# Routed experts computed in split bf16, with the weights split during the dense attention

## The reference, cut to what matters

```
x = x + dense cross attention(layernorm(x), context of 4 x 1601 rows; 16 query heads, 4 KV heads of 128)
x = x + (routed experts + shared expert)(layernorm(x))
x = x + window attention(layernorm(x))
x = x + fp8 feed forward(layernorm(x))
```

```
scores = sigmoid(x @ gate_w); the best 2 of 4 groups of experts, in these the best 6 of 32 experts for each token
xs = the 1024 * 6 rows of x, sorted by expert
g = ragged_dot(xs, w_gate); u = ragged_dot(xs, w_up)          # 256 x 176 for each expert
d = ragged_dot(silu(g) * u, w_down)                           # 176 x 256 for each expert
out = sum over the 6 experts of a token, weighted, + silu(x @ sw_gate) * (x @ sw_up) @ sw_down
```

## Time and profile before

| what | value |
|---|---|
| median of 3 executions | 1865.14 us (1864.81 to 1865.66) |
| the profiled execution | 1864.89 us, span 1862.8 us |
| PE busy, share of the span | 1710.4 us, 92% |
| DVE | 1405.2 us, 75% |
| ACT | 1103.7 us, 59% |
| POOL | 1100.0 us, 59% |

### The profile page before, as it was taken

How to read it: one execution, slowest core, us unless ns; L and a number is a source line. 1 busy time by engine, 2 the same in 40 slices (tenths; PEclk the granted TensorE clock), 3 DMA queues, 4 the chain that set the end, 5 groups by cost and what they waited for, 6 DMA issues and landing times. The chain is left out here.

```text
span 1862.8 us, 41598 instructions
## 1 busy us (share of the span) xinstructions
PE 1710.4 (92%) x14581; PEld 1314.5 (71%) x14727; DVE 1405.2 (75%) x3734; ACT 1103.7 (59%) x2798; POOL 1100.0 (59%) x1718
## 2 busy tenths in 40 slices
PE   4799999999999999999999999986999999589987
PEld 3578777788787787877787887765555555339974
DVE  7898886888877878888788788756656665575746
ACT  6576777676777667777676666652134333173534
POOL 5578695786866958868568577510266664181210
PEclk8899999999999999999999999996999999796998
DMA  3211111011010100110001000325389996500100
GB/s 126 75 52 30 61 39 50 19 36 47 18 39 19 37 20 18 59 32 19 19 19 36 24 1 24 122 92 220 101 253 269 275 267 188 189 15 24 43 9 26
DMA packets 69529, 140.24 MB, mean 75 GB/s; under 512 B 10921, under 2 KB 38674, under 8 KB 69074
## 3 DMA queue, kind: packets, MB, share of 16 engines
q1 hardware_dynamic: 58514, 105.37, 18.3%
q0 software_dynamic: 9984, 30.42, 4.8%
q10 hardware_dynamic: 832, 1.84, 0.3%
HBM read 111.73 MB, written 25.86 MB: 74 GB/s over the span
## 5 line engine op out<-in xcount | busy, mean ns | idle before, releaser
L920 DVE TENSOR_TENSOR att_pT<-att_pT 128x512 bf16<-128x512 f32 (+1 forms) x512 | 320.9, 650 | 166.2 <-ACT att_pT L729 163.1
L565 PE MATMUL att_out<-att_V,att_pT 128*128 128x128 bf16 x5760 | 386.8, 219 | 13.9 <-DVE att_pT L920 12.0
L565 PEld LDWEIGHTS att_out<-att_V,att_pT 128*128 128x128 bf16 x5760 | 349.0, 98 | 40.8 <-DVE att_pT L920 24.3
L729 ACT ACTIVATE att_pT<-att_pT 128x512 bf16<-128x512 f32 (+1 forms) x512 | 278.0, 572 | 128.8 <-PE att_pT L551 128.8
L735 ACT ACTIVATE att_prob<-att_scores,att_negmax 128x512 f32<-128x512 f32 (+1 forms) x512 | 330.3, 655 | 17.5 <-DVE att_negmax L909 16.9
L542 PE MATMUL att_scores<-att_K,att_Q 128*128 128x512 bf16 (+1 forms) x1408 | 298.5, 359 | 7.2 <-DVE att_Q L881 0.5
L907 DVE TENSOR_REDUCE att_mx<-att_scores 128x1 f32<-128x512 f32 (+1 forms) x512 | 291.0, 629 | 1.0 <-PE att_scores L542 0.9
L551 PE MATMUL att_pT<-att_ident,att_prob 128*128 128x128 f32 x1920 | 274.2, 274 | 0.0
L542 PEld LDWEIGHTS att_scores<-att_K,att_Q 128*128 128x128 bf16 x1536 | 150.6, 98 | 144.1 <-issue 1.9
L551 PEld LDWEIGHTS att_pT<-att_ident,att_prob 128*128 128x128 f32 x1920 | 208.6, 141 | 0.8
L465 PE MATMUL att_aux<-att_wkv,att_kvT 128*128 128x256 bf16 x1350 | 167.2, 273 | 17.8 <-DVE att_aT L881 15.2
(11 more groups left out here) (347 smaller groups left out, 3250.6 us busy)
## 6 DMA issues: line engine op xcount, KB each, us to landing
moe_wa<-in_wa_l SPq DMA_DIRECT2D x80, 480.0 KB
att_wq<-wq_s SPq DMA_DIRECT2D x12, 512.0 KB, 3.7
att_wo<-wo_s SPq DMA_DIRECT2D x12, 512.0 KB, 3.8
att_stage<-in_ctx_l SPq DMA_DIRECT2D x9, 512.0 KB, 4.3
near_s<-att_windows POOLq DMA_DIRECT2D x8, 576.0 KB, 5.5
win_near<-near_s SPq DMA_DIRECT2D x32, 144.0 KB
moe_wb<-in_wb_l SPq DMA_DIRECT2D x80, 48.0 KB
moe_wa<-y_s SPq DMA_DIRECT2D x5, 768.0 KB, 11.0
```

Source lines behind the costliest of these rows:

```text
L565: last = nc.tensor.matmul(out_ps[:, i % 2, :], pT[:, i % 2, a, k, :], V[:, par, k, w, :], start=(k, a, w) == (0, 0, 0), stop=(k, a) == (KT ...
L729: nc.scalar.activation(pT[:, i % 2, 0, 4 * j:4 * j + m, :], pT_ps[j % 2][:, 0:m, :], ACT.Copy).then_inc(s["pt_hi"], 1)
L920: nc.vector.tensor_tensor(pT[:, i % 2, 1, 4 * j:4 * j + m, :], pT_ps[j % 2][:, 0:m, :], pT[:, i % 2, 0, 4 * j:4 * j + m, :], ALU.subtract) ...
```

## The change: what it does

1. The weights of the 32 routed experts come as one f32 array of 128 x 1056 for each expert (`we_l`, 528 KB). 32 new split jobs ("we") cut them into bf16 halves during the dense attention, one expert each. They stand in slots 0, 2, 6, 7 of groups 3, 7, 11, 12, 13 and 14, in slots 2 and 6 of groups 4 and 8, and in slots 0 and 7 of groups 5 and 9. All 32 use one buffer for the two halves (`halves_out`, the second buffer of `windows`); two DMAs store it, to `wu_s` and `wd_s`, and the high half of the next job waits until both have landed (`expert_out`). The layer norm of the next batch moves from that buffer to the first one of `windows`, and on DVE behind the step of the angles.
2. The 80 tiles load both bf16 halves (three DMAs instead of two, the same bytes) and compute each product as high x high + high x low + low x high: six bf16 matmuls for gate and up, six for down. ACT writes the high halves of the turned rows and of the turned hidden rows, DVE the low ones. The shared expert stays in f32.
3. `quantize` does one operation of 576 columns after each tile instead of ten of 144 columns after every second one. The loads at the end have six places instead of seven, three of them in `w8`, and wait for the last step of `quantize`.

```
+SPLIT_E, SPLIT_W = 32, 1056
+EXPERT_AT = [(g, i) for g in range(3, GROUPS - 1) for i in ((0, 2, 6, 7) if g % KVH == 3 or g > 12 or g == 12 else ((2, 6), (0, 7), ())[g % KVH])]
+JOBS_AT = sorted(JOBS_AT + [(at, ("we", e)) for e, at in enumerate(EXPERT_AT)], key=lambda x: x[0])
...
+        halves_out = flat[:, 1, :].bitcast(BF16)[:, 0:2 * SPLIT_W].rearrange("p (a n) -> p a n", a=2)
...
                     sp.wait_ge(s["split_lo"], j + 1)
+                    if job[0] == "we":
+                        sp.dma_start(t["wu_s"][job[1]], halves_out[:, :, 0:DC * GU]).then_inc(s["expert_out"], 16)
+                        sp.dma_start(t["wd_s"][job[1]].rearrange("a (p n) -> p a n", p=P), halves_out[:, :, DC * GU:SPLIT_W]).then_inc(s["expert_out"], 16)
+                        return
...
+                    elif job[0] == "we":
+                        wait(act, s["expert_out"], 32 * job[1])
...
-                    sp.dma_start(wa[:, u, :], t["wa_l"][bass.ds(e, 1)].rearrange("e p n -> p (e n)")).then_inc(load[u], 16)
-                    sp.dma_start(wb[:, u, :], t["wb_l"][bass.ds(e, 1)].rearrange("e p n -> p (e n)")).then_inc(load[u], 16)
+                    down = t["wd_s"][bass.ds(e, 1)]
+                    sp.dma_start(wu[:, u, :, :], t["wu_s"][bass.ds(e, 1)].rearrange("e p a n -> p (e a) n")).then_inc(load[u], 16)
+                    sp.dma_start(wd[:, u, :, :], down[:, :, 0:P * D].rearrange("e a (p n) -> p (e a) n", p=P)).then_inc(load[u], 16)
+                    sp.dma_start(we[:, u, :, :], down[:, :, P * D:M * D].rearrange("e a (p n) -> p (e a) n", p=REST)).then_inc(load[u], 16)
...
+                        for c in range(DC):
+                            for a, w in ((0, 0), (0, 1), (1, 0)):
+                                last = nc.tensor.matmul(up, xT[:, i % 3, a, c, :], wu_flat[:, first + (w * DC + c) * GU:first + (w * DC + c) * GU + GU],
+                                                        start=(c, a, w) == (0, 0, 0), stop=(c, a) == (DC - 1, 1))
...
+                def hidden_high(i):
+                    act.wait_ge(s["ht_done"], SHARED + i + 1)
+                    wait(act, s["y_done"], SHARED + i - 2)
+                    nc.scalar.activation(hT[:, i % 3, 0, :, :], ht_ps[i % 2][:, 0:2, :], ACT.Copy).then_inc(s["ht_hi"], 1)
...
+                def rows_low(i):
+                    dve.wait_ge(s["xt_hi"], i + 1)
+                    V.tensor_tensor(xT[:, i % 3, 1, :, :], xt_ps[i % 2][:, 0:DC * P].rearrange("p (c n) -> p c n", c=DC), xT[:, i % 3, 0, :, :],
+                                    ALU.subtract).then_inc(s["xt_lo"], 1)
```

More of the change, by code:

```diff
@@ L285, in staged @@
                 return home[:, 0:DC * n].rearrange("p (c k) -> p c k", c=DC)
-            return home[:, 0:512 if job[0] == "wkv" else 1024]
+            return home[:, 0:{"wkv": 512, "we": SPLIT_W}.get(job[0], 1024)]
         def split_to(job, a):
@@ L407, in _ @@
                             sp.wait_ge(wo_stored[u], 16)
-                        sp.wait_ge(s["late_stored"], 16 * sum(job[0] != "ctx" and job not in (("wo", 0), ("wo", 1)) for job in SPLITS))
+                        sp.wait_ge(s["late_stored"], 16 * sum(job[0] in ("wkv", "wq", "wo") and job not in (("wo", 0), ("wo", 1)) for job in SPLITS))
                         sp.dma_start(wkv[:, par, :, :, :].rearrange("p a c n -> p (a c n)"), t["wkv_s"][late % KVH]).then_inc(load[par], 16)
@@ L995, in extra @@
                             token_stats(b + 1)
+                        for k in TRIG_AT.get(at, ()):
+                            trig_step(b + 1, k)
                         if at == NORMALISE_AT:
                             normalise(b + 1)
-                        for k in TRIG_AT.get(at, ()):
-                            trig_step(b + 1, k)
                     if (g, i) in SPLIT_AT:
@@ L1155 @@
 E_ALL, TOPK, GRP, TOP_GRP = 32, 6, 4, 2
-M = 176
 EXPERTS = E_ALL + 2
-GU = 2 * M
 REST = M - P
 WA = DC * GU + D
+REST_W = M * D // P
+assert SPLIT_E == E_ALL and SPLIT_W == DC * GU + REST_W
 NSLOT = 80
@@ L1513, in gate_up @@
                     wait(pe, s["h_done"], j - 1)
-                    if i >= 0:
-                        pe.wait_ge(s["xt_sb"], i + 1)
-                        pe.wait_ge(load[i % WRING], 32 * (i // WRING + 1))
-                    for c in range(DC):
-                        rows = xT[:, i % 3, c, :] if i >= 0 else h32[:, c, j // 2 * P:(j // 2 + 1) * P]
-                        w = wa[:, i % WRING, :] if i >= 0 else shared_a[:, j % 2, :]
-                        last = nc.tensor.matmul(up_ps[j % 2][:, 0:GU], rows, w[:, c * GU:(c + 1) * GU], start=c == 0, stop=c == DC - 1)
+                    up = up_ps[j % 2][:, 0:GU]
+                    if i < 0:
+                        for c in range(DC):
+                            last = nc.tensor.matmul(up, h32[:, c, j // 2 * P:(j // 2 + 1) * P], shared_a[:, j % 2, c * GU:(c + 1) * GU], start=c == 0, stop=c == DC - 1)
+                    else:
+                        first = i % WRING * (2 * DC * GU)
+                        pe.wait_ge(s["xt_lo"], i + 1)
+                        pe.wait_ge(load[i % WRING], 48 * (i // WRING + 1))
+                        for c in range(DC):
+                            for a, w in ((0, 0), (0, 1), (1, 0)):
+                                last = nc.tensor.matmul(up, xT[:, i % 3, a, c, :], wu_flat[:, first + (w * DC + c) * GU:first + (w * DC + c) * GU + GU],
+                                                        start=(c, a, w) == (0, 0, 0), stop=(c, a) == (DC - 1, 1))
                     last.then_inc(s["up_done"], 1)
@@ L1524, in turn_hidden @@
                     pe.wait_ge(s["h_done"], j + 1)
-                    wait(pe, s["ht_sb"], j - 1)
+                    wait(pe, s["ht_lo"], j - 1)
                     for c in range(2):
@@ new lines, in quantize @@
+                    w = w8[:, part]
+                    wait(dve, s["quant"], step)
+                    if k == 0:
+                        ins = V.tensor_scalar(magic[:, :].bitcast(I32), w.bitcast(I32), 0x7F800000, None, ALU.bitwise_and)
+                    elif k == 1:
+                        ins = V.tensor_scalar(magic[:, :], magic[:, :], 2.0 ** -6, 1.5 * 2 ** 20, ALU.max, ALU.mult)
+                    elif k == 2:
+                        ins = V.tensor_tensor(y8[:, :], w, magic[:, :], ALU.add)
+                    elif k == 3:
+                        ins = V.tensor_tensor(y8[:, :], y8[:, :], magic[:, :], ALU.subtract)
+                    elif k == 4:
+                        ins = V.tensor_scalar(over[:, :], y8[:, :], E4M3_MAX, 3e38, ALU.is_gt, ALU.mult)
+                    elif k == 5:
+                        ins = V.tensor_scalar(magic[:, :], y8[:, :], -E4M3_MAX, 3e38, ALU.is_lt, ALU.mult)
+                    elif k == 6:
+                        ins = V.tensor_tensor(over[:, :], over[:, :], magic[:, :], ALU.add)
+                    elif k == 7:
+                        ins = V.tensor_scalar(over[:, :], over[:, :], 10.0, None, ALU.mult)
+                    elif k == 8:
+                        ins = V.scalar_tensor_tensor(y8[:, :], y8[:, :], 1.0, over[:, :], ALU.mult, ALU.add)
+                    else:
+                        ins = V.tensor_tensor(wq_flat[:, part], y8[:, :], over[:, :], ALU.subtract)
@@ L1724, in _ @@
                         shares(j - SHARED - 4)
[L1725 to L1730 removed]
+                    if j == SHARED:
+                        dve.wait_ge(s["w8_in"], 16)
+                    if SHARED <= j < JOBS:
+                        quantize(j - SHARED)
                 dve.wait_ge(s["share_step"], 3 * TOPK)
```

116 lines of the change are left out of this document (64 added, 52 removed).

## The result

The changed kernel takes 1916.28 us (median of four, 1912.55 to 1918.97), the kernel before 1865.40 us in the same comparison: 1.027 times as long, 95% interval 1.025 to 1.0289, some 51 us more. The forecast was 1880 us with a range up to 1902: the sign was right, the size not. The profiled execution took 1917.32 us (span 1915.5, mean granted clock 0.949 where it was 0.961).

The account below looks back on a forecast made before the run. The prediction took PE to bound attention and experts, with POOL limiting the changed tiles. From 1864.9 us it added 49 us for the attention and subtracted 33 us for the experts: 1881, stated as 1880 us, range 1856 to 1902.

Parts of the forecast that it names:

- PE bounds both stages: Attention and expert tiles: PE sets the end of both, busy 72.14 of 74.14 us and 231.66 of 232.31 us.
- SP's order delays slot 2: Attention, slot 2 of eight groups: load and stores issue behind SP's wait for WO 1; PE loses 4.0 us each, 32 us.
- The bound: Attention, slot 2 of eight groups: range of the forecast stall, from shortest to longest landing times, 10 to 47 us.
- The fourth rival: Attention, slot 2: stalls of 6 us as loads and stores land near their longest times; 1896 us, chance 0.09.
- Slot 6: Attention, eight groups: DVE's low half stands ahead of the sum PE needs; 1.5 us each, 12 us (8 to 14).
- Slots 7 and 0: Attention: low half exceeds DVE's idle time, 3 us; next job waits for stores from the one halves buffer, 2 us.
- POOL sets the tile: Expert tiles: a scatter and gather pair costs 2.56 us, taken as 2.60 per tile for 69 tiles.
- PE waiting for the gathered rows: Expert tiles: sign expected in the changed kernel's profile, beside a pitch of 2.6 us.
- The last eleven tiles: End of the experts: about 11 tiles go at PE's pace, 2.20 us instead of 2.94, winning 8.1 us.
- SP's third issue: Expert tiles: two issues start 0.54 us apart; a third adds that much again and fits into 2.6 us.
- the second rival: Expert tiles go at 2.87 us, from slow DMA packets or POOL's DMAs waiting for DVE; 1900 us, chance 0.14.
- The rule of the Trainium skill: Expert tiles: DVE's long tensor_scalar steps could delay POOL's DMAs, 0.3 us a tile; not counted in the sum.

## Why the prediction was wrong, step by step

- **PE bounds both stages; SP's order delays slot 2.** Right in mechanism and place: the eight groups named are the eight that stall, groups 4 and 8 don't, and taking SP's order away takes the stall away. The step that failed is the size of this term, "PE loses 4.0 us [...] 8 x 4.0 = 32 us". It measured 56.1 us. Of this, 40.7 us are put down to the wait (5.1 a group). The sum let the stores land 4.2 us behind their issue, beside the load; in group 13 the second one landed 5.8 us behind its own, since the weights, the key table with its tables and the load for slot 6 were on the way as well: DMA had a share of 0.95 from 1112 to 1117 us. The other 15.4 us are the clock, which stood in no term: the kernel before has no wait of PE of this length in the attention, and its 1.00 was taken as given behind waits of 4 us.
- **The bound was drawn from landing times alone.** 10 to 47 us held the wait, but not the wait and the clock together. The missing 36 us are 24 in slots 1 and 2, some 9 that the tiles won less, and some 4 in the other slots. The fourth rival, stores that land near their longest times, came nearest, and it too left out the clock.
- **Slot 6**, 12 us: measured 13.2. **Slots 7 and 0**, 3 + 2 us: 7.9 with all else. Slot 7 is 0.9 to 1.5 us longer in groups 5, 9 and 11 to 13, and 1.4 in group 2 by the clock; slot 0 of groups 12 to 14 is no longer than before.
- **POOL sets the tile**, 2.56 us a pair: right, 2.57 in clean stretches. The way was another than the sign "PE waiting for the gathered rows": it leads through the landing of the scatters. The value taken, 2.60, became 2.68, as the gathers grew by 0.10 us: 5.4 of the 33 us. The last eleven tiles won 5.8 instead of 8.1 in this trace.
- **SP's third issue "fits into 2.6":** right, and barely: the sum had the issues alone, and with the reading of the expert's number a round takes 2.3 to 2.6 us. SP is the second bound.
- **DMA's share near 0.9 as a bound** (the second rival): wrong. With a third of the weights' bytes gone the tile stayed at 2.66 us (a share of 0.82) and, with half the gathers, at 2.46 (0.75); at 0.96 with two issues no tile waited for a load.
- **The rule of the Trainium skill** weighed there ("SBUF — State Buffer", the "DVE blocks DMA" trap, on tensor_scalar): the traces show it weakly, 1.01 to 1.06 us against 0.97 (the prediction counts six such steps of ten; there are five). The same page of the Trainium skill, section "Who interferes with whom", has a VectorE instruction with two SBUF inputs contend with a GpSimd instruction that reads SBUF, but reports that tensor_tensor did not stall a DMA. Here that form goes with the longest gathers, 1.22 us on the mean, and in the run without it none takes over 1.21, so for these DMAs the traces speak against that; the run without such steps gained no time, so that a price of it is not shown.

## What to carry to other kernels

Work that fits into an engine's idle time is free only if its data is there: before a job is added, follow its load and its stores through the issuing queue, past every wait that stands ahead of them. Transfers that are issued together are to be priced together, not each by its median. A wait that stops PE for several microseconds is to be priced with the slower clock that can follow, here about 2 us on top of 5. And where the bounding engine is relieved, list the time per item of every engine left, issuing queues included: POOL at 2.57, SP at 2.4 and PE at 2.24 us stood within 15% of each other.

## What the runs showed of the hardware

The granted clock stood at 0.50 (1.2 GHz) for 3.4 or 6.8 us at each of the eight waits of the changed kernel (3.4 to 5.4 us), and stayed up in the five groups where the same time was filled with products. Behind waits of 1.9 to 3.9 us, in the run with the load alone first, it fell in three groups of six; behind the three short waits in slot 7 of group 2 it fell in the changed kernel and not in the kernel before. A share of busy DMA engines of 0.96, at 300 GB/s, delayed no tile, once SP issued two loads in place of three. In the attention the second store landed 5.6 to 6.6 us behind its issue at the stalled place of the eight groups, where other transfers were on the way (share 0.95 in group 13); its median over all 32 jobs is 3.0. SP's three issues with their register work took mostly 2.3 to 2.6 us. POOL's indirect DMAs of 128 rows took 0.97 us a gather and 0.99 a scatter, with 0.30 us between.
